# Softmax norm of layer 1 taken apart over three engines, all q.k products on one engine, and a new written order with more filler matmuls

## The reference

```python
# attention among the batches, at each position (L0 ffn)
scores = jnp.einsum('nhld,nhmd->nhlm', q, k) / np.float32(np.sqrt(HD))
attn = jax.nn.softmax(scores, axis=-1)
o = jnp.einsum('nhlm,nhmd->nhld', attn, v)
...
# experts: tokens beyond cap per expert are dropped
y1 = _ln(x + _mha(...)); y2 = _ln(y1 + _moe(y1, ...))
```

## Time and profile before

| | us |
|---|---|
| median of 3 runs | 551.32 |
| all runs | 551.32, 551.1, 556.45 |
| the profiled execution: time | 555.6 |
| the profiled execution: span | 553.8 |
| VectorE busy in it | 481.4 |
| TensorE busy in it | 431.9 |
| ScalarE busy in it | 291.3 |
| GpSimd busy in it | 277.4 |

### The profile page before, as it was taken

One profiled execution on the slowest core, in us unless ns is written; L12 is line 12 of the kernel. 1 busy time (PEld: TensorE's weight loads), 2 busy tenths in 40 slices (PEclk: granted clock), 3 DMA queues, 4 the chain that ended last, 5 costly groups with the idle time before them and its releaser, 6 DMA issues. The chain is left out here.

```text
span 553.8 us, 10801 instructions
## 1 busy us (share of the span) xinstructions
PE 431.9 (78%) x2655; PEld 325.0 (59%) x2655; DVE 481.4 (87%) x3014; ACT 291.3 (53%) x797; POOL 277.4 (50%) x400
## 2 busy tenths in 40 slices
PE   4989997797896886878977987877876976765285
PEld 4569865566655663656655655655654754553274
DVE  4954679959868798999899999999999999999971
ACT  1225551323443435424877688787777687544333
POOL 4410141504327447535575578668648567554612
PEclk9999998978996999899989899878778889556768
DMA  9600000000000000000000000000000000000000
GB/s 279 290 1 1 2 1 1 1 2 0 2 2 0 2 2 0 2 0 2 7 6 2 5 2 2 11 1 1 11 1 7 1 7 6 2 10 2 5 5 11
DMA packets 5933, 9.60 MB, mean 17 GB/s; under 512 B 744, under 2 KB 4976, under 8 KB 5616
## 3 DMA queue, kind: packets, MB, share of 16 engines
q1 hardware_dynamic: 5584, 8.35, 4.3%
q10 hardware_dynamic: 288, 0.56, 0.3%
HBM read 7.86 MB, written 1.05 MB: 16 GB/s over the span
## 5 line engine op out<-in xcount | busy, mean ns | idle before, releaser
L959 DVE MAX8 top<-area_b 128x8 f32<-128x77 f32 x768 | 112.8, 222 | 0.0
L967 DVE MATCH_REPLACE8 area_b<-top,area_b 128x77 f32<-128x77 f32 x512 | 106.9, 222 | 0.0
L1283 PE MATMUL psT<-consts,p 128*128 128x128 f32 (+1 forms) x160 | 35.1, 348 | 33.8 <-POOL p L444 27.0
L1331 PE MATMUL psT<-mrow,mones 128*128 128x308 bf16 x314 | 53.3, 309 | 1.4 <-ACT pT L516 0.8
L967 DVE MATCH_REPLACE8 area_b<-top,area_a 128x77 f32<-128x77 f32 x256 | 53.5, 223 | 0.0
L1299 PE MATMUL psM<-vblk,pT 128*128 128x135 f32 (+3 forms) x320 | 48.8, 316 | 3.2 <-ACT pT L652 2.6
L1299 PEld LDWEIGHTS psM<-vblk,pT 128*128 128x128 f32 (+1 forms) x320 | 46.5, 225 | 7.6 <-issue 7.2
L1102 PE MATMUL psM<-vblk,pT 128*128 128x135 f32 (+3 forms) x320 | 44.2, 296 | 7.8 <-ACT early L579 4.5
L1283 PEld LDWEIGHTS psT<-consts,p 128*128 128x128 f32 (+1 forms) x160 | 23.1, 174 | 44.4 <-POOL p L444 29.4
L1102 PEld LDWEIGHTS psM<-vblk,pT 128*128 128x128 f32 (+1 forms) x320 | 41.4, 204 | 11.3 <-issue 9.8
L598 ACT ACTIVATE mparts<-psM,cur 128x128 f32<-128x128 f32 x128 | 38.1, 368 | 9.4 <-PE psM L1239 9.3
(11 more groups left out here) (224 smaller groups left out, 1050.6 us busy)
## 6 DMA issues: line engine op xcount, KB each, us to landing
area_a<-in_w1T SPq DMA_DIRECT2D x1, 2064.0 KB, 11.2
area_b<-in_w SPq DMA_DIRECT2D x1, 2048.0 KB, 15.5
x<-in_x SPq DMA_DIRECT2D x4, 256.0 KB, 6.9
out<-fin SPq DMA_DIRECT2D x16, 64.0 KB, 1.6
rows<-in_rows SPq DMA_DIRECT2D x1, 576.0 KB, 7.0
vblk<-in_vblk SPq DMA_DIRECT2D x1, 540.0 KB, 15.9
weights<-in_weights SPq DMA_DIRECT2D x1, 516.0 KB, 6.7
consts<-in_consts ACTq DMA_DIRECT2D x1, 392.5 KB, 4.0
```

The lines of the kernel that those rows point to most:

```text
L959: ins = e.max(tops[:, r, h], (left if r else scores_sb[t % RING])[:, h])
L967: ins = e.match_replace(left[:, h], tops[:, r, h], (left if r else scores_sb[t % RING])[:, h], GONE)
L1283: ins = tr(psT[0:w, 0, (c % 4) * P:(c % 4 + 1) * P], p1[:, c * P:c * P + w], ident)
L1331: mm(bank[:, 0:B * KEYS], mones[:], mrow.rearrange("p b k -> p (b k)"), start=True, stop=True)
```

## The change

Four things change.

1. **The division of layer 1**, for the tiles 0 to 14. VectorE keeps the reciprocal (`norm@t`). ScalarE copies the 128 value columns out of the bank into a new tile `avs` (`acopy@t`). GpSimd multiplies `avs` with the reciprocals (`aproduct@t`), ahead of `add3@t`. TensorE's next `value` waits for the copy and the reciprocal rather than for the product. Tile 15 keeps the old form.
2. **The products among the batches** are all VectorE's: `qk2`, `qk3` and `wv3` leave GpSimd.
3. **217 fills and 60 stokes** in place of 157 and 10, and a stoke waits only for the last scores to be kept, not for the top-k of the last tile.
4. **The string ORDER is written anew** from end to end.

```diff
-QKG = 2
-WVG = 3
-FILLS = 157
-STOKES = 10
+FILLS = 217
+STOKES = 60
...
+        avs = sb("avs", [P, H, HD])
...
             def value(t):
+                def product():
+                    hold(e, s["a_copied"], t + 1)
+                    hold(e, s["a_den"], t + 1)
+                    hold(e, s["x3_set"], t)
+                    e.tensor_tensor(att1.rearrange("p (h d) -> p h d", h=H), avs[:], rden1[:, :, None].broadcast_to([P, H, HD]), ALU.mult)\
+                        .then_inc(s["a_norm"], 1)
...
-                return dict(add3=d) if t < LASTT else dict(root=root)
+                return dict(aproduct=product, add3=d) if t < LASTT else dict(root=root)
...
+            def value(t):
+                def aside():
+                    hold(e, s["a_den"], t + 1)
+                    hold(e, s["a_norm"], t)
+                    e.activation(avs[:], pv1[:, :, 0:HD], ACT.Copy).then_inc(s["a_copied"], 1)
+                return dict(acopy=aside) if t < LASTT else {}
...
             def value(t):
+                def inverse():
+                    hold(e, s["a_made"], t + 1)
+                    hold(e, s["a_norm"], t)
+                    e.reciprocal(rden1[:], pv1[:, :, HD]).then_inc(s["a_den"], 1)
...
-                return dict(norm=a) if t < LASTT else dict(norm=a, close=close, closen=norm)
+                return dict(norm=inverse) if t < LASTT else dict(norm=a, close=close, closen=norm)
...
-                            hold(e, s["a_norm"], t)
+                            hold(e, s["a_copied"], t)
+                            hold(e, s["a_den"], t)
...
                 def after():
                     hold(e, s["S_kept"], NT)
-                    hold(e, s["topk_step"], TOPK_STEPS * NT - (STOKES - (k - FILLS)) + 1)
+
                     stream(psS[:, G - 1])
...
-ORDER = """hstats@0 masks@0 hrstd@0 kblk1@0 hnorm@0 vb0@0 kblk@0 hturn@0 bias@0 vb1@0 hT@0 vm0@0 hq@0 keys@0 hstats@1 hqT@0 vm1@0 hrstd@1 s0@0
...
+ORDER = """hstats@0 masks@0 hrstd@0 kblk1@0 hnorm@0 vb0@0 kblk@0 hturn@0 vb1@0 keys@0 hT@0 bias@0 vm0@0 hq@0 hstats@1 hqT@0 vm1@0 s0@0
```

More of the change, by code:

```diff
@@ L1395 @@
-max13@2 scale4@0 exp@2 mark10@2 norm4@0 mark11@2 fturn@0 shift@0 turn0@1 load@4 mark12@2 sum2@3 up@0 square2@3 mark13@2 copy0@1
-scale2@3 max20@2 turn1@1 acts@0 max21@2 half@0 down@0 norm2@3 max22@2 copy1@1 affine@3 turn@4 copy@4 max23@2 turn2@1 mark20@2 sum3@3
-moe0@4 copy2@1 mark21@2 square3@3 fvalue@0 value@1 scale3@3 gated0@4 mark22@2 end@0 mark23@2 norm3@3 max30@2 max31@2 lturn@3 moe1@4
-lT@3 norm@1 max32@2 add3@1 ask@3 gated1@4 max33@2 cut@2 qT@3 fill@125 fill@126 moe2@4 sum4@1 scores@3 square4@1 gated2@4 total@4
@@ L1407 @@
-fill@140 fill@141 turn0@3 exp@4 mark11@4 moe1@6 half@2 mark12@4 sum3@5 end@2 square3@5 mark13@4 copy0@3 scale3@5 gated1@6 fill@142
-fill@143 turn1@3 max20@4 max21@4 norm3@5 fill@144 moe2@6 max22@4 gated2@6 lturn@5 max23@4 lT@5 total@6 copy1@3 mark20@4 mark21@4
-mark22@4 ask@5 mark23@4 qT@5 turn2@3 load@7 sum2@6 scores@5 square2@6 max30@4 copy2@3 max31@4 scale2@6 value@3 keep@5 max32@4 keys@6
-max33@4 norm2@6 max00@5 cut@4 max01@5 max02@5 turn@7 max03@5 copy@7 mark00@5 dif@5 fill@145 moe0@7 sign@4 norm@3 mark01@5 mark02@5
@@ new lines @@
+fill@178 fill@179 fill@180 turn@5 mark12@3 turn1@2 copy@5 mark13@3 end@1 sum3@4 moe0@5 copy1@2 max20@3 square3@4 turn2@2 max21@3
+gated0@5 scale3@4 max22@3 copy2@2 fill@181 fill@182 fill@183 moe1@5 max23@3 norm3@4 mark20@3 lturn@4 value@2 gated1@5 mark21@3 lT@4
+mark22@3 mark23@3 ask@4 moe2@5 norm@2 max30@3 qT@4 gated2@5 fill@184 scores@4 acopy@2 max31@3 aproduct@2 max32@3 total@5 keep@4
+add3@2 max33@3 keys@5 cut@3 sum4@2 max00@4 square4@2 max01@4 sum2@5 max02@4 square2@5 max03@4 scale4@2 sign@3 mark00@4 load@6
@@ new lines @@
+max01@6 norm@4 fvalue@3 max02@6 moe1@8 cut@5 acopy@4 norm3@7 max03@6 lturn@7 mark00@6 lT@7 gated1@8 ask@7 mark01@6 aproduct@4 qT@7
+mark02@6 add3@4 scores@7 sign@5 dif@6 mark03@6 moe2@8 max10@6 max11@6 sum4@4 square4@4 max12@6 product@5 gated2@8 max13@6 keep@7
+total@8 mark10@6 mark11@6 scale4@4 mark12@6 exp@6 turn0@5 mark13@6 load@9 norm4@4 keys@8 sum2@8 end@3 max20@6 fturn@4 shift@4
+max21@6 square2@8 up@4 copy0@5 max22@6 scale2@8 max23@6 turn1@5 acts@4 mark20@6 norm2@8 half@4 down@4 copy1@5 mark21@6 affine@8
@@ new lines @@
+max13@8 aproduct@6 mark10@8 exp@8 turn0@7 add3@6 mark11@8 scale2@10 sum4@6 square4@6 mark12@8 norm2@10 scale4@6 mark13@8 copy0@7
+turn@11 turn1@7 affine@10 norm4@6 max20@8 copy1@7 max21@8 fturn@6 keys@10 shift@6 max22@8 turn2@7 end@5 sum3@10 up@6 max23@8
+square3@10 copy@11 mark20@8 scale3@10 copy2@7 moe0@11 acts@6 mark21@8 half@6 norm3@10 down@6 mark22@8 lturn@10 fvalue@6 value@7
+lT@10 mark23@8 end@6 gated0@11 max30@8 max31@8 max32@8 ask@10 moe1@11 max33@8 qT@10 norm@7 max00@9 scores@10 cut@8 gated1@11 max01@9
@@ new lines @@
+gated1@12 up@7 mark23@9 acts@7 ask@11 moe2@12 max30@9 qT@11 half@7 max31@9 down@7 gated2@12 scores@11 copy2@8 max32@9 fvalue@7
+total@12 end@7 max33@9 keep@11 max00@10 keys@12 max01@10 cut@9 max02@10 max03@10 value@8 sum2@12 mark00@10 square2@12 load@13 sign@9
+dif@10 mark01@10 mark02@10 mark03@10 scale2@12 max10@10 norm@8 max11@10 product@9 norm2@12 acopy@8 max12@10 turn@13 max13@10 copy@13
+mark10@10 moe0@13 mark11@10 affine@12 gated0@13 turn0@9 mark12@10 aproduct@8 sum3@12 mark13@10 moe1@13 square3@12 add3@8 sum4@8
@@ L1471 @@
+part3@15 value0@15 add3@14 sum4@14 turn1@15 square4@14 copy1@15 scale4@14 turn2@15 value1@15 norm4@14 copy2@15 fturn@14 shift@14
+value2@15 up@14 norm@15 close@15 acts@14 root@15 down@14 fvalue@14 half@14 closen@15 end@14 fturn@15 shift@15 up@15 acts@15 half@15
+down@15 end@15""".split()
 def kernel(**inputs):
```

269 lines of the change are left out of this document (120 added, 149 removed).

## The result

| | before | changed |
|---|---|---|
| median, us | 553.34 (20 runs) | 557.43 (20 runs) |
| all runs, us | 547.67 to 557.53 | 550.81 to 559.81 |
| the profiled execution, time / span | 555.6 / 553.8 | 559.8 / 557.9 |

The ratio is 1.0072, 95% interval 1.0038 to 1.0106: the changed kernel is 0.7% slower, some 4 us, where my sum said 11 us faster and my forecast was 542 us. The ratios leave out the runs that lie more than 1.5% above the fastest of their kernel, 6 of the changed kernel's 20 (its profiled execution is one of them), 5 of e14's 12, 7 of e11's 12 and 3 of e10's 6.

What follows compares the result with a forecast made beforehand. VectorE was taken to bound the middle, TensorE the stretch from 42 to 56 us. The terms -3.4 - 1.2 - 3 + 0 - 3.6 gave -11.2 us, forecast 542 us; own range 534 to 546 (chance 0.71), 8 in 10 for 533 to 551.

Steps and rivals of the forecast that it cites:

- They cost nothing while that slack covers them: Split norm, tiles 0 to 13: -3.4 us on VectorE; added ScalarE copies and GpSimd products taken as 0 (0 to +2).
- Fillers in the middle: 43 more pairs up to the load of tile 8, standing at TensorE's waits: 0 us, ends -3 and +3.
- the rival of the overrunning fillers: Between `proj@3` and the scores of tiles 3 to 7, 86 exposed fill matmuls slow the kernel to 560 us; chance 0.07.
- There one microsecond off VectorE is one off the span: Middle of the kernel: VectorE, busy 26.93 of 27 us, bounds; other engines' work is free until it delays VectorE's inputs.
- the five terms: Norm -3.4, products among the batches -1.2, start -3, fillers in the middle 0, end -3.6; together -11.2 us.
- The start: Before the experts' products, value products move into time of fillers and waits: -3 us, ends 0 and -5.
- The products: Products among the batches all on VectorE, without meeting GpSimd's: 26.3 us instead of 27.5, -1.2 us, ends -3 and +3.
- The end: Tiles 14 and 15: earlier cut of tile 14, `turn0@15` 5.4 us earlier, clock charged 1 us: -3.6 us, ends 0 and -6.
- The port rule: GpSimd and VectorE lock a shared port pair, so 15 GpSimd products could give back 6.8 us; decided against.
- The last tile cold: Rival, last tile: without stokes its transposes leave the clock low, +3 on 542, 545 us; part of the 0.71.
- nothing to be seen: Rival: start gives nothing, end only what the lower clock leaves; within 1%, 546.1 to 548 us; chance 0.22.
- The change does not do what it says: Rival: GpSimd's product comes late and holds VectorE's reciprocal, which waits for `a_norm` of the tile before; 0 us, not counted.

Runs made afterwards that it cites:

- e14: e5 plus one GpSimd product per tile that nobody reads, ahead of each residual; ratio 0.9874 to the kernel before.
- e11: Changed kernel with 43 fewer fills between the first maxima of tile 0 and the load of tile 8; ratio 1.0042 to the kernel before.
- e10: Changed kernel with GpSimd's copy of the experts' result of tiles 10 and 11 behind the product of tiles 7 and 8; ratio 1.0107 to the kernel before.
- e2: e1 with the split norm in addition, old order, old fills and stokes; ratio 1.0146 to the kernel before.
- e1: Kernel before with all products among the batches on VectorE, old order, norm whole; ratio 1.0053 to the kernel before.
- e12: e5 with the split norm in addition; ratio 1.0049 to the kernel before.
- e5: Kernel before with new order up to the first maxima of tile 0, old behind, all products on VectorE, norm whole; ratio 0.9891 to the kernel before.
- e3: Changed kernel with the norm whole on VectorE again, new order, fills and stokes kept; ratio 1.0068 to the kernel before.
- e6: Kernel before with only the new order up to the first maxima of tile 0, products still shared with GpSimd; ratio 0.9888 to the kernel before.
- e16: e5 with the new order from the first maxima of tile 13 on and 60 stokes, norm whole; ratio 0.985 to the kernel before.
- e8: Changed kernel with GpSimd's last mix steps behind the cut, for tiles 7 to 9, 11, 13 and 14; ratio 1.0293 to the kernel before.
- e9: Changed kernel with norm, copy, product and residual of tiles 6 to 9 and 11 some 5.6 us later in the order; ratio 1.0274 to the kernel before.
- e20: e5 with new order from tile 8's first maxima, 60 stokes, but six TensorE steps and partners at their old places; ratio 1.0129 to the kernel before.
- e4: Changed kernel (split norm) with everything after the first maxima of tile 8 in the old order, 10 stokes; ratio 1.0024 to the kernel before.

## Why the prediction was wrong, step by step

- **"They cost nothing while that slack covers them; without it the residual of each tile is 0.7 us later, and the first thing late is `mix`, not the top-k."** The failed step. I read ScalarE's and GpSimd's 19.6 of 27 us busy as slack. In the old order the split cost 5.1 us (e2 against e1) and 8.7 (e12 against e5), where the forecast had -3.4. The 0.7 us were the durations of copy and product; the hand-over was 4.4 us more at tile 12, and its wait stands in a queue in order. That `mix` is late first was right, but the next cut stands behind `mix` on GpSimd, and the values behind the cut, so it did reach the top-k. Nothing of it shows as a busy engine: e14, with as much GpSimd work and no hand-over, lost nothing clear of the noise.
- **"Fillers in the middle: 0."** The second failed step: I priced the fills of the new order and not the order. With the norm whole, the new order behind the start costs 0.0177, 9.8 us (e3 against e5), at most some 1.7 of them by the fills (e11). For the rival of the overrunning fillers that is all there is, far from its price; the mean clock of 0.81 that I cited for it is of 374 to 401 us, while in the place it names, tiles 3 to 7, the laps before read 0.82 to 1.00. The string moved experts, mix, values and transposes against each other on four engines in tiles 0 to 12; I looked at the start and the end.
- **"There one microsecond off VectorE is one off the span"** holds only while what VectorE reads is ready well ahead. At tile 7 it was not. TensorE's values and VectorE's norm, in the kernel before:

```profile
394.13 2.49 PE L1299 MATMUL psM<-vblk,pT 128*128 128x81 f32 x20
```

```profile
396.76 0.24 DVE L992 RECIPROCAL rden<-psM 128x16 f32<-128x16 f32 x1
```

  The values end at 396.62 and the norm begins at 396.76, 0.14 us later. The lead from the start does not use this up. e5 begins its top-k 5.2 us earlier (177.78), and the same norm still waits for nothing:

```profile
387.96 2.48 PE L1285 MATMUL psM<-vblk,pT 128*128 128x81 f32 x20
```

```profile
390.57 0.26 DVE L978 RECIPROCAL rden<-psM 128x16 f32<-128x16 f32 x1
```

  The values hang on VectorE's own maxima by the loop and move with them. What the 0.14 us say is that a step more on that way, or a later place in a queue, is at once a wait of VectorE: 3.13 us at this tile in e12, 4.96 in the changed kernel.
- **The two together** are not additive: 8.7 and 9.8 us alone, 10.0 with both (changed kernel against e5). My reading, which no run tests: whatever makes the loop longer eats the same slack, and where VectorE is no longer the bound its 3.4 us are worth nothing.
- **The range.** I wrote that all ends together reach -17 and -5. The ends that I had given to the five terms add up to -20.4 and +4.6, and the measured +4.0 (0.0072 of 553.3) lies just inside. The range was narrower than its own terms.
- **The start**, -3 (0 to -5): -6.2 us by e6 (-4.1 to -8.3), right in sign, and beyond my end. Sign in the trace: first maxima 5.0 us earlier.
- **The products**, -1.2: 0 by e5 and e6, +2.9 by e1, inside the ends. VectorE's two groups take 11.0 and 16.6 us in the changed kernel; I had 9.8 and 16.5.
- **The end**, -3.6: in e16 the ratio fell by 0.004 (2.3 us), with overlapping intervals. Its trace says so more plainly: from the first maxima of tile 15 to the end are 38.9 us, 41.7 in e5, 41.5 before. So with the norm whole the mechanism holds in part, though the cut of tile 14 starts 3.8 us after its maxima and not 0.1. In the changed kernel, 42.0, it gave nothing. "The cut starts at 512.4" took `norm@12`'s place in VectorE's queue for the time of the residual; on GpSimd the new product of tile 12 stood behind the product of tile 13. "VectorE no longer waits" missed that its first part needs the last transposes of tile 14 done, and `turn0@15` came 1.6 us after the two parts and not 0.3, behind the values of tile 14.
- **The port rule.** e14's 15 products on GpSimd gave back nothing, 0.9874 against 0.9891, so I was right not to pay the 6.8 us. But I had taken the rule too widely. The section (the Trainium skill, "SBUF — State Buffer", section "SBUF: two separate sides") names the VectorE instructions that meet the lock: those in a two-port mode, and those with two inputs in SBUF. The maxima have one input. The rows agree on both kinds: 16 maxima take 2.34 us beside GpSimd's difference and 2.31 without, while VectorE's products of q and k, which have two, take 1.09 us in the mean before and 0.69 in e1, where GpSimd has none of them.
- **The last tile cold** (the Trainium skill, "TensorE: Matmul & The Clock Gate", section "Part 4: PE-mode transpose"): the transposes of tile 14 ran at the lower level (granted clock 0.50 from 528 to 537 us), 1.12 us for four, and the 20 values behind them took 2.63 us, near the 2.48 of the higher level; the clock reads 1.00 from 538 us on. Between the pause and its rise TensorE ran eleven transposes, ten plain matmuls of the mix and the first of the values, so no run here shows whether transposes count. The rival came in part: from `turn0@15` to the end are 17.4 us at a mean granted clock of 0.72, before 15.2 at 0.89, where I had 16.0 and 1 for the clock. From the first two parts of the last tile to the end are 19.0 us, inside the 16 to 20 that I gave. It is not where most was lost.
- **The rivals.** The outcome lies within 1%, where I had 0.22, but that is luck and not "nothing to be seen": its start was to give nothing, and the start gave most. "The change does not do what it says" came nearest. It asked for `a_norm` alone, where the product of the tile before is indeed long done, and not for who waits behind the copy.
- **My own signs of error** were waits for kept scores over 5 us (5.1 us measured, of which 3.6 were there before) and maxima over 0.16 us (0.147 measured). Neither points at the loss: I had named no sign for the values.

Open: which places of the new order cost what. Each of three stretches carries a part, and no attempt to move single places made anything better (e8, e9, e10, e20). Open also how much of the split's price hangs on the granted clock, and whether the products on VectorE cost 0 or 3 us.

## What to carry to other kernels

An engine that is busy 70% of the time is not free when its queue is in order: price a hand-over by what stands ahead of it in the receiver's queue and follow the result once round the loop, back to the engine that bounds. Where an engine is busy 26.9 of 27 us, ask how much earlier its inputs were ready; here, at tile 7, the answer was 0.14 us. And an order that is rewritten as a whole is an unknown of its own, to be tried in stretches: here the start gained 6 us and the end perhaps 2, and the middle lost more.

## What had not been expected of the hardware

Part of the scatter of the kernels with the new start is made in their first 22 us. The changed kernel and e4 have the same instructions up to tile 8. The first maximum of the scores, of the one and the other:

```profile
22.08 1.44 DVE L716 TENSOR_REDUCE mx<-psS 128x16 f32<-128x1232 f32 x1 [4.22 <-PE psS L1059]
```

```profile
16.98 1.43 DVE L716 TENSOR_REDUCE mx<-psS 128x16 f32<-128x1232 f32 x1
```

and two matmuls ahead of it:

```profile
16.65 1.97 PE L1043 MATMUL psM<-hT,early 128*128 128x512 f32 x2
```

```profile
13.51 1.05 PE L1043 MATMUL psM<-hT,early 128*128 128x512 f32 x2
```

The same matmuls take nearly twice as long, the ratio of TensorE's two levels of 1.2 and 2.4 GHz (four transposes take 1.11 and 0.60 us at them), although the granted clock reads 1.00 from 0 to 20 us in both. The 5.1 us are kept: the first maxima of tile 0 start at 177.95 and 171.99. The other traces with the new start fall the same way, from 177.66 to 179.26 where the two matmuls take 1.97 us (nine traces), and from 171.99 to 173.53 where they take 1.05 (seven; the eighth, e3, has 176.41). With the old start the slow pair costs little: 182.98 us before with 1.97, 182.18 in e1 and 180.94 in e2 with 1.05. So against the old start the new one is 5 us ahead where this pair is slow, and some 7 to 10 where it is fast.

That is not all of the scatter. Behind the first maxima of tile 0, e2 and e12 issue the same steps in the same order, but for five that fell on the other side of that point, and took 373.5 and 380.2 us from there to the end. The granted clock was 0.91 and 0.73 between tile 6 and tile 7, and 0.75 and 0.65 from the first maxima of tile 15 on, which took 40.6 and 44.2 us. Single runs must not be compared here, and with the split neither must the time from a fixed point to the end.
